# Reordering the work inside a slot of a software-pipelined causal attention

## The reference

```python
h = rmsnorm(x, ln1_w)                       # x: 4 sequences of 256 tokens, 256 wide
q = rope(h @ Wq)                            # 32 heads of 128
k = rope(h @ Wk); v = h @ Wv                # 4 key/value heads of 128, each for 8 query heads
scores = where(causal, q @ k.T / sqrt(128), -1e9)
attn = softmax(scores)
x = x + (attn @ v) @ Wo
```

## Time and profile before

| | |
|---|---|
| median of 3 runs | 1281.88 us (1279.15 to 1282.68) |
| the profiled execution | 1281.74 us, span 1279.9 us, mean granted clock 0.907 |
| TensorE busy | 1086.9 us, 85% of the span |
| VectorE busy | 889.4 us, 69% |
| ScalarE busy | 591.8 us, 46% |
| GpSimd busy | 373.5 us, 29% |
| the chain that ended last | TensorE 68%, VectorE 11%, ScalarE 7%, GpSimd 5%, issue 5% |

### The profile page before, as it was taken

The page is one execution under the profiler, slowest core; times in us unless marked ns, Lnnn a source line. Parts: engine busy times, 40 slices in busy tenths (PEclk is TensorE's granted clock), DMA queues, the critical chain, the costliest instruction groups (busy, mean ns, idle before and its releaser), DMA issues.

```text
span 1279.9 us, 20165 instructions
## 1 busy us (share of the span) xinstructions
PE 1086.9 (85%) x6066; PEld 866.5 (68%) x6074; DVE 889.4 (69%) x2600; ACT 591.8 (46%) x1547; POOL 373.5 (29%) x315
## 2 busy tenths in 40 slices
PE   7988898419999316889999989998998999999998
PEld 3555555415666205778887878887887888888887
DVE  4788777615776186667667676767675878878877
ACT  5656546103333114766666666666566322222221
POOL 1655545040000333323232223222110233323331
PEclk9868776658999757999999999999998899999999
DMA  7900000111111310111000101000000111111111
GB/s 248 324 1 1 1 1 1 61 66 37 47 45 47 98 54 0 38 38 34 1 9 34 34 1 30 2 1 1 2 1 14 38 42 44 49 49 49 49 42 41
DMA packets 55568, 53.56 MB, mean 42 GB/s; under 512 B 5520, under 2 KB 48976, under 8 KB 55488
## 3 DMA queue, kind: packets, MB, share of 16 engines
q1 hardware_dynamic: 53952, 48.38, 12.1%
q0 software_dynamic: 1536, 4.20, 1.0%
HBM read 43.38 MB, written 9.18 MB: 41 GB/s over the span
## 4 chain that ended last, share of the span: by engine, by line
PE 68%; DVE 11%; ACT 7%; POOL 5%; issue 5%; DMA 1%; SPq 0%; DVEq 0%; ACTq 0%; POOLq 0%
PE bank L56 11%; PE bank L57 11%; PE bank L58 11%; PE bank L802 4%; PE bank L581 4%; PE bank L712 3%; PE bank L720 3%; PE bank L737 3%; PE bank L823 3%; PE bank L812 3%; POOL rot_s L1216 3%; PE bank L564 2%; ACT swap L1034 2%; ACT swap L1033 2%; DVE g_scale L1319 2%
## 5 line engine op out<-in xcount | busy, mean ns | idle before, releaser
L1216 POOL TENSOR_TENSOR rot_s<-swap,rq 128x512 f32<-128x512 f32 x64 | 82.3, 1287 | 236.5 <-ACT swap L1034 236.5
L1047 ACT ACTIVATE prob<-prob,pmin 128x128 f32<-128x128 f32 (+1 forms) x256 | 114.4, 448 | 40.7 <-DVE pmin L1624 38.4
L952 ACT ACTIVATE silu<-bank 128x512 f32<-128x512 f32 x66 | 39.6, 599 | 178.0 <-PE bank L58 178.0
L1643 DVE TENSOR_TENSOR o_ring<-bank,o_ring 128x256 fp32r<-128x256 f32 x128 | 53.9, 421 | 85.3 <-ACT o_ring L1063 85.3
L802 PE MATMUL bank<-kv,norm 128*128 128x128 f32 (+1 forms) x512 | 107.4, 333 | 3.5 <-DVE norm L1617 3.2
L1513 DVE SCALAR_TENSOR_TENSOR xs<-bank,wt,xs 128x256 f32<-128x256 f32 x264 | 109.1, 476 | 0.0
L812 PE MATMUL bank<-ident,prob 128*128 128x128 f32 x384 | 65.7, 280 | 49.8 <-DVE prob L1636 44.7
L1162 POOL TENSOR_TENSOR gate_r<-gate_w,gate_r 128x256 fp32r<-128x256 f32 x33 | 38.9, 1177 | 222.3 <-ACT gate_r L938 222.3
L1063 ACT ACTIVATE o_ring<-bank 128x256 fp32r<-128x256 f32 x128 | 48.4, 378 | 116.8 <-PE bank L824 116.8
L1636 DVE TENSOR_SCALAR prob<-prob,pinv 128x128 f32<-128x128 f32 (+1 forms) x256 | 93.9, 407 | 4.5
L1144 POOL TENSOR_SCALAR rest<-alpha 128x512 f32<-128x512 f32 x32 | 69.2, 2164 | 80.1 <-ACT alpha L884 78.8
(11 more groups left out here) (240 smaller groups left out, 3148.5 us busy)
## 6 DMA issues: line engine op xcount, KB each, us to landing
gate_w<-in_Wg SPq DMA_DIRECT2D x33, 128.0 KB, 2.1
up_w<-in_Wu SPq DMA_DIRECT2D x33, 128.0 KB, 2.2
down_w<-in_Wd SPq DMA_DIRECT2D x33, 128.0 KB, 2.2
w_all<-in_w_gate SPq DMA_DIRECT2D x8, 512.0 KB, 10.5
w_all<-in_w_up SPq DMA_DIRECT2D x8, 512.0 KB, 10.5
w_all<-in_w_down SPq DMA_DIRECT2D x8, 512.0 KB, 10.4
wq_g<-in_Wq SPq DMA_DIRECT2D x4, 1024.0 KB, 5.1
wo_g<-in_Wo SPq DMA_DIRECT2D x4, 1024.0 KB, 5.3
```

Source lines behind the costliest of these rows:

```text
L1047: ins = act.activation(prob[:, u % 4, nt * P:nt * P + (nt + 1) * P], prob[:, u % 4, nt * P:nt * P + (nt + 1) * P], ACT.Exp, bias=pmin[:, u ...
L1216: pool.tensor_tensor(rot_s[:, m % 2].rearrange("p (b n) -> p b n", b=2), swap[:, m % 2].rearrange("p (b n) -> p b n", b=2), bcast(tab[:, 1 ...
```

## The change

On each of three engines two steps inside a slot change places. On TensorE the weighted sum goes ahead of the output product. On ScalarE the copy of the transposed probabilities goes ahead of the exponentials. On VectorE the normalising and the sum of the rotary embedding go ahead of the product with the cosines. Every instruction, buffer and wait stays, and SyncE's and GpSimd's programs are the same.

```diff
@@ TensorE, in attention()
+                    if 0 <= k - 3 < AU:
+                        weigh(k - 3)
                     if 0 <= k - 5 < AU:
                         project_out(k - 5)
-                    if 0 <= k - 3 < AU:
-                        weigh(k - 3)
@@ ScalarE
                     if (q := job_in(k, 1)) is not None:
                         swap_halves(*q)
+                    if 0 <= k - 2 < AU:
+                        copy_T(k - 2)
                     if 0 <= k < AU:
                         exps(k)
-                    if 0 <= k - 2 < AU:
-                        copy_T(k - 2)
@@ VectorE
                     if 0 <= k - 4 < AU:
                         low_out(k - 4)
-                    if (q := job_in(k, 1)) is not None:
-                        cosines(*q)
                     if 0 <= k - 1 < AU:
                         normalise(k - 1)
                     if (q := job_in(k, 2)) is not None:
                         rotate(*q)
+                    if (q := job_in(k, 1)) is not None:
+                        cosines(*q)
```

## The result

The changed kernel takes 1226.18 us (median of 4 runs) against 1282.28: a ratio of 0.957, 95% interval 0.9546 to 0.9595. (One of the four runs before was in a slower state at 1354.09 us and is left out of the ratio; the median of the other three is 1281.88.) The forecast was 1224.6 with a range of 1218 to 1246. The profiled execution took 1225.96 us, span 1223.9, so the span is 56.0 us shorter than before.

The account below looks back on a forecast made before the run. TensorE was taken as the bound, held by `turn` waiting for VectorE's normalising in short slots. Seven block sets at 7.6 us (53.2), 2.3 in the first block and 1.6 at the start: 57.1 off 1281.74 gives 1224.6 us, range 1218 to 1246.

Parts of the forecast that it names:

- What bounds: Attention blocks: TensorE's `turn` waits six times a block for VectorE's normalising; without waits 59.98 becomes 52.4 us.
- VectorE's edit: Short slots: normalising ends at T+1.5, not T+3.3, ahead of `sines`; T is when `weigh` is seen finished.
- TensorE's edit: Short slots: `project_out` behind `weigh` makes `turn` due at T+2.75, not T+2.05; 1.25 us slack with VectorE's edit.
- ScalarE's edit: Short slots: `copy_T` ends at T+2.1, not T+3.0; cover without own term, bounds nothing to 0.25 us each.
- `rotate`: Slot before each block's start: wait for `rotate` goes, 0.25 us a block; `sines` held up to 0.45 us, without cost.
- The ramp: First block: 2.3 us from slots 6 and 8, plus 1.6 taken at the start, bounds 0 to 2.5.
- The two whole waits: First block, short slots 6 and 8: their `turn` waits go, 1.05+1.26 = 2.3 us.
- the place of `cosines`: Attention's start: `cosines` (511.88) stands ahead of the normalising that `turn` at 513.46 awaits, 0.6 us.
- the 1.0 us of slot 3: Ramp, short slot from `turn` at 513.46 to 516.84: 3.38 us instead of 2.35, counted as 1.0 us.
- the normalising doesn't meet `sines`: Rival, short slots: `sines` starts first, normalising ends at T+3.3, 0.55 us late; 1249 or 1234 to 1249; chance 0.18.
- The wait did not move to `weigh`: Rival: `weigh` waits for `copy_T` or `low_out`, or VectorE's recurrence sets the pace, 1281.7 us; chance 0.04.
- The clock did not fall: Rival, attention: granted clock falls when small gaps go; at 0.8 the kernel takes 1326 us; chance 0.03.

Follow-up runs that it names:

- 0.9 us of delay: Whole change plus a VectorE memset of 128 x 1024 ahead of the normalising in each short slot: 1248.89 us, ratio 0.9748.
- the short delay: Whole change plus a VectorE memset of 128 x 512 ahead of the normalising in each short slot: 1234.57 us, ratio 0.9645.
- the second moved version: Whole change with `split_activations(1, 1)` moved out of slot 1 and the first four ScalarE and GpSimd weight pieces moved: 1222.43 us, ratio 0.9527.

## Why the prediction was right

- *What bounds:* six waits of `turn` a block, for the normalising. Right: they are gone, and the block is the 52.4 us of TensorE's own work that was summed from the chain (52.39).
- *VectorE's edit:* the normalising was to end at T+1.5, ahead of `sines`; it does. Wrong was the side remark that this edit alone would leave 0.55 us of slack. It left out the second thing that `turn` waits for, `copy_T` at T+3.0, though the number stood one paragraph further on. Alone the edit is worth 13.3 us of attention, where by the remark it would have been nearly all of it.
- *TensorE's edit:* `turn` due 0.70 us later. Right: 0.55 us of wait is left with it alone (0.6 forecast). Not seen was how little it adds once the other two are there, 4.8 us. And the slack of 1.25 us counted the normalising alone: with `copy_T` at T+2.12 it is 0.64.
- *ScalarE's edit:* cover with no term of its own, 0.25 us a short slot if missing. Right: 0.24.
- *`rotate`:* its wait ahead of each block was to go; it went. What the prediction worked out from the Trainium skill ("SBUF — State Buffer", Who interferes with whom) came true: `rotate` now holds up `sines` (1.57 us in slot 14) at no cost. The other side of the same rule was missed: were it not ahead of `sines`, it would be held itself, and TensorE with it, 3.2 us of attention.
- *The ramp:* 1.6 and 2.3 us forecast, 1.0 us measured together. Cut at the starts of `turn`, the ramp falls into these parts, from the first value product to the second:

| part | before | after | gained | forecast |
|---|---|---|---|---|
| up to `turn` of slot 3 | 26.59 | 25.80 | 0.8 | 0.6 |
| slot 3 | 3.38 | 3.60 | -0.2 | 1.0 |
| slot 4 | 3.08 | 4.92 | -1.8 | 0 |
| slot 5 to the second value product | 16.02 | 13.72 | 2.3 | 2.3 |

The two whole waits and the place of `cosines` were sized well. The mis-sized term is the 1.0 us of slot 3: the prediction took away the wait that it saw and did not ask what the normalising would meet when it came earlier. (Nor is 2.35 us the work of that slot: no unit is yet due for its output product of 0.70.) The rows of the changed kernel, with the two multiplications of the normalising apart:

```profile
512.05 1.27 POOL L1204 TENSOR_TENSOR wo_r<-wo_g,wo_r 128x512 fp32r<-128x512 f32 x1 [3.25 <-ACT wo_r L1041]
512.36 1.04 DVE L1636 TENSOR_SCALAR prob<-prob,pinv 128x128 f32<-128x128 f32 x1
513.27 1.27 POOL L1216 TENSOR_TENSOR rot_s<-swap,rq 128x512 f32<-128x512 f32 x1
513.32 1.37 DVE L1636 TENSOR_SCALAR prob<-prob,pinv 128x256 f32<-128x256 f32 x1
...
514.75 0.50 PEld L812 LDWEIGHTS bank<-ident,prob 128*128 128x128 f32 x3 [1.26 <-DVE prob L1636]
519.67 0.36 PEld L812 LDWEIGHTS bank<-ident,prob 128*128 128x128 f32 x3
```

The normalising, moved earlier, now lands behind a weight product of GpSimd and then behind `sines`: 2.33 us in all, where it took 0.87 before (515.92). Slot 4 was in no term. Its columns as in the earlier trace rows, before and after:

```profile
516.84:519.92 3.08, 3.08 (x17) 2.71 (x18) 3.04 (x13) 2.10 (x8) 1.65 (x2) 0.96 0.08 14
514.75:519.67 4.92, 4.92 (x17) 4.16 (x18) 3.81 (x15) 2.40 (x8) 2.06 (x2) 0.58 0.36 114
```

TensorE has the same 17 products and is busy all the time in both, so the 1.8 us are the clock's (length times clock is 3.0 and 2.9): 0.96 before, 0.58 after, which is the lower level, 1.2 GHz, for most of the slot. TensorE had stood 4.63 us ahead of slot 3 and 1.26 ahead of slot 4; before, it stood 5.43 and 0.37, and the low clock fell on slot 3 (0.53). In the second profile of the changed kernel, after waits of 4.64 and 0.43, slot 4 takes 3.83 us at 0.76, which is most of the 1.3 us by which its ramp is shorter. So this part varies by itself.

- *The rivals:* the normalising doesn't meet `sines` in the blocks; with 0.9 us of delay it does, at the price set. The wait did not move to `weigh`. The clock did not fall in the blocks: 1.00 at 100% busy.

Not shown: what sets the start of the attention between 479.5 and 487.9 us, and what decides on which slot of the ramp the lower clock falls.

## What to carry to other kernels

In a software pipeline written out in slots, work out for each waiting step of the bounding engine all of its releasers with their time in the slot, not just the one that the table of waits names: here the second stood 0.3 us behind the first, and VectorE's edit alone stopped there, at 13 of 54 us. On an in-order engine, a step that waits for something late in the slot (the swap) belongs behind steps whose input is already there. And a step can be made early enough for its reader and still be lost if it starts just behind a product of GpSimd, as `rotate` did with the short delay and the normalising did in the ramp.

## What the runs showed of the hardware that I had not expected

- How sharp the edge is: `rotate` 0.27 us ahead of `sines` takes 0.68 us, 0.23 us behind it 1.78. The normalising takes 0.55, 0.86, 1.35 or 2.33 us by what GpSimd does.
- Two products in a row on GpSimd hold VectorE twice: the normalising's two multiplications each got through behind one of them (1.04 and 1.37 us in the ramp of the changed kernel, 0.79 and 1.38 in that of the second moved version; both together take 0.55 where nothing is in the way).
- VectorE's memset of 128 x 1024 (0.91 us from 596.66) and the start of `sines` at 597.34 overlap without either being stretched: the memset of half the size takes 0.48 where it meets nothing, and `sines` keeps its 1.29.
- TensorE at 100% busy for seven blocks (536 to 903 us of the changed kernel) has a granted clock of 1.00 throughout, whereas in the ramp a wait of 4.6 us was followed by a slot at 0.63 and one at 0.58 in one profile, and by 0.50 and 0.76 in another of the same kernel.
